# Layer 1's second-half queries projected densely and spread by four transfers, with steps 8 and 9's scores behind the transposed scores of steps 4 and 5

## What is computed

```python
x = x + L0_xattn(layernorm(x), ctx)   # 16 heads of 8
x = x + L0_ffn(layernorm(x))          # 8 experts, the best one for each token
x = x + L1_xattn(layernorm(x), ctx)   # 16 heads of 8, as below
x = x + L1_ffn(layernorm(x))          # 8 experts, the best two, gelu

q = (query @ Wq + bq); k = (key_value @ Wk + bk); v = (key_value @ Wv + bv)   # 16 heads of 8
attn = softmax(clip(q k^T * scale, -CLAMP, CLAMP))
attn = where(any(isnan(attn)), 1 / Nkv, attn)
out = (attn v) @ Wo + bo
```

## Time and profile before

| | us |
|---|---|
| median of 3 runs | 232.23 (232.05 to 233.31) |
| the profiled execution | 231.29 |
| its span in the trace | 229.5 |

### The profile page before, as it was taken

One profiled execution on the slowest core, in us unless ns is written; L12 is line 12 of the kernel. 1 busy time (PEld: TensorE's weight loads), 2 busy tenths in 40 slices (PEclk: granted clock), 3 DMA queues, 4 the chain that ended last, 5 costly groups with the idle time before them and its releaser, 6 DMA issues.

```text
span 229.5 us, 6728 instructions
## 1 busy us (share of the span) xinstructions
PE 212.9 (93%) x2522; PEld 168.8 (74%) x2522; DVE 161.1 (70%) x516; ACT 120.1 (52%) x225; POOL 75.7 (33%) x100
## 2 busy tenths in 40 slices
PE   8999987998779999999979899999699999999994
PEld 8666866766458999999875657877568686776774
DVE  1785765877556865577538755798758965799995
ACT  6765554665725655656510386567563275343340
POOL 8820810010530577646351394666600100000000
PEclk9999999999999999999999799999999999999999
DMA  6932118582244016120211110212200000001001
GB/s 216 365 110 51 50 41 276 169 282 85 58 114 95 24 60 175 50 80 26 67 51 48 50 49 28 74 50 71 76 1 0 3 0 0 3 1 46 1 3 46
DMA packets 14116, 17.18 MB, mean 75 GB/s; under 512 B 1684, under 2 KB 10004, under 8 KB 14084
## 3 DMA queue, kind: packets, MB, share of 16 engines
q1 hardware_dynamic: 11732, 13.59, 19.8%
q0 software_dynamic: 1152, 2.24, 3.2%
q10 hardware_dynamic: 1200, 0.92, 1.3%
HBM read 11.18 MB, written 3.95 MB: 66 GB/s over the span
## 4 chain that ended last, share of the span: by engine, by line
PE 71%; DVE 13%; DMA 5%; ACT 3%; issue 3%; POOL 2%; DVEq 0%; POOLq 0%; SPq 0%; ACTq 0%
PE ps L1219 12%; PE ps L1443 12%; PE ps L1455 12%; PE ps L1529 6%; PE ps L1539 5%; PE ps L1278 4%; PE ps L1227 2%; PE ps L1489 2%; DVE mx L785 2%; DVE xn L749 2%; PE ps L1316 2%; PE ps L1292 2%; PE ps L1247 2%; DMA q<-work 2%; PE ps L1180 2%
## 5 line engine op out<-in xcount | busy, mean ns | idle before, releaser
L785 DVE TENSOR_REDUCE mx<-ps 128x4 f32<-128x512 f32 x64 | 41.1, 685 | 19.7 <-PE ps L1219 19.3
L577 ACT ACTIVATE PT<-ps 128x512 f32<-128x512 f32 x64 | 35.6, 590 | 25.9 <-PE ps L1227 25.9
L1219 PE MATMUL ps<-k,q 32*128 32x128 f32 x512 | 37.0, 288 | 4.1 <-DMA q<-mT 1.2
L1219 PEld LDWEIGHTS ps<-k,q 32*128 32x128 f32 x512 | 31.4, 191 | 12.6 <-DVE mx L785 9.7
L1455 PEld LDWEIGHTS ps<-proj,work 128*128 128x128 f32 x256 | 30.7, 192 | 5.7 <-issue 5.7
L713 ACT ACTIVATE work<-ps,fc 128x512 f32<-128x512 f32 x32 | 21.4, 687 | 24.0 <-PE ps L1443 22.5
L1227 PE MATMUL ps<-q,k 32*128 32x128 f32 x512 | 33.6, 288 | 0.3 <-DVE mx L785 0.3
L1455 PE MATMUL ps<-proj,work 128*128 128x128 f32 x256 | 31.1, 275 | 0.0
L445 POOL DMA_INDIRECT moe_y<-ys,tok_i x22 | 22.3, 1012 | 24.0 <-DVE ys L1018 12.0
L1443 PE MATMUL ps<-xT,fc 128*128 128x512 f32 x64 | 30.1, 593 | 0.0
L1227 PEld LDWEIGHTS ps<-q,k 32*128 32x128 f32 x512 | 28.2, 191 | 1.0 <-issue 0.7
(11 more groups left out here) (169 smaller groups left out, 292.5 us busy)
## 6 DMA issues: line engine op xcount, KB each, us to landing
fc<-in_fc SPq DMA_DIRECT2D x8, 256.0 KB, 3.6
proj<-in_proj SPq DMA_DIRECT2D x8, 256.0 KB, 4.2
slots_x<-xs SPq DMA_DIRECT2D x2, 709.5 KB, 7.5
fc<-in_w SPq DMA_DIRECT2D x8, 129.0 KB, 2.2
proj<-in_w SPq DMA_DIRECT2D x8, 128.0 KB, 2.5
k<-work SPq DMA_DIRECT2D x12, 64.0 KB
wr<-in_wr SPq DMA_DIRECT2D x1, 719.5 KB, 7.6
xs<-slots_x SPq DMA_DIRECT2D x2, 322.5 KB, 4.0
```

The source lines that it names most:

```text
L577: nc.scalar.activation(PT[:, j % PTR, :], ps[:, ST_BANK(layer, j), :], ACT.Exp, scale=SCALE).then_inc(b_done, 1)
L785: nc.vector.tensor_reduce(mx[:, b, 4 * g:4 * g + 4], ps[:, S_BANK(layer, j), :].rearrange("p (k m) -> p k m", m=M), axis=AX, op=ALU.max).t ...
L1219: ins = mm(ps[:, S_BANK(layer, 2 * n + i), P * k:P * k + P], q4[r:r + 32, k, L * b:L * b + L], k4[r:r + 32, k, M * b:M * b + M], start=Tru ...
```

## The change

The second-half queries of layer 1 (rows 4 to 7) are projected by one dense product in step 8, evacuated once to `q_dense[:, 1, :]`, and spread by four DMAs, two issued by SP (behind the maxima of row 2) and two by ACT (behind the evacuation). In steps 8 and 9 the scores are held back: the transposed scores 4 and 5 run alone, and the scores of 8 and 9 follow behind transposed scores 5, one after the other. DVE does norm(8, 0) ahead of tops(16), and guard_count ahead of tops(18). The zero rows of q4 for rows 4 to 7, which the spaced product wrote, come by one more DMA from SP. The weights of layer 1's experts are issued one row later from expert 1 on. `wq` and `bq` of layer 1 leave the weights wr (516 columns), and qk_sums and tn2 go from 7 to 4 columns.

```diff
@@ RING
                 if layer == 1 and n == 8:
-                    for i in range(4, 8):
-                        RING[1]["q", i] = len(RING[1])
+                    RING[1]["q"] = len(RING[1])
...
+        def last_queries_in(queue, lo, hi):
+            queue.wait_ge(b_done, ring_no(1, "q"))
+            for g in range(lo, hi):
+                queue.dma_start(q4[32 * g:32 * g + DH, :, N // 2:N], q_dense[32 * g:32 * g + 32, 1, :]).then_inc(q_in[2], 16)
@@ SP, shift_rows
-                    if layer == 1 and b >= 1:
-                        expert_weights(b - 1)
+                    if layer == 1 and b == 2:
+                        last_queries_in(sp, 0, 2)
+                    elif layer == 1 and b >= 1:
+                        expert_weights(b - 1 if b < 2 else b - 2)
@@ SP
             second_keys_in(1)
+            sp.dma_start(q4[DH:P:32, :, N // 2:N], zero_rows[:]).then_inc(q_zeroed, 16)
             slots_in(1)
...
             shift_rows(1)
+            expert_weights(E - 2)
             expert_weights(E - 1)
@@ ACT
-            def queries_evac_ring(i):
-                act.wait_ge(q_ps, Q_DONE[1] + i - 3)
-                nc.scalar.activation(q4[:, i - 4, 512:1024], ps[:, ring_at(1, ("q", i)), :], ACT.Identity,
-                                     bias=wcol(1, "bq")[:, i - 4:i - 3],
-                                     accum_out=qk_sums[:, i - 1:i]).then_inc(b_done, 1)
+            def last_queries_evac():
+                act.wait_ge(q_ps, Q_DONE[1] + 1)
+                nc.scalar.activation(q_dense[:, 1, :], ps[:, ring_at(1, "q"), :], ACT.Identity, bias=wcol(1, "bqd"),
+                                     accum_out=qk_sums[:, 3:4]).then_inc(b_done, 1)
...
                     if layer == 1 and n == 8:
-                        for i in range(4, 8):
-                            queries_evac_ring(i)
+                        last_queries_evac()
+                        last_queries_in(act, 2, 4)
                         o_evac(0)
@@ DVE
                 for n in range(LAST):
+                    if layer == 1 and n == 8:
+                        norm(8, 0)
+                    if layer == 1 and n == 9:
+                        guard_count()
                     tops(2 * n)
...
-                    if layer == 1 and n == 9:
-                        guard_count()
...
-                    if n in O_T:
+                    if n in O_T and (layer, n) != (1, 8):
                         norm(n, O_T[n])
@@ PE
             def second_queries():
                 pe.wait_ge(ln_xT, XT_NO(2, 1))
-                for i in range(4, 8):
-                    pe.wait_ge(b_done, ring_no(1, ("q", i)) - 3)
-                    mm(ps[:, ring_at(1, ("q", i)), :], wcol(1, "wq")[:, P * (i - 4):P * (i - 4) + P], xT[:, 512:1024],
-                       start=True, stop=True).then_inc(q_ps, 1)
+                pe.wait_ge(b_done, ring_no(1, "q") - 3)
+                mm(ps[:, ring_at(1, "q"), :], wcol(1, "wqd"), xT[:, 512:1024], start=True, stop=True).then_inc(q_ps, 1)
...
                     if layer == 1 and n == 0:
-                        pe.wait_ge(q_zeroed, 16)
+                        pe.wait_ge(q_zeroed, 32)
                         pe.wait_ge(q_in[1], 64)
+                    if layer == 1 and n == 8:
+                        pe.wait_ge(q_in[2], 64)
...
+                def scores_alone(n):
+                    scores(n)
+                    for k in range(4):
+                        for i in range(2):
+                            score(n, i, k)
...
-                    if n < 2 * B:
+                    held = layer == 1 and n in (8, 9)
+                    if n < 2 * B and not held:
                         scores(n)
                     alone = layer == 1 and m == 0
                     if 0 <= m < 2 * B and not alone:
                         scores_t(m)
                     for k in range(4):
                         for i in range(2):
-                            if n < 2 * B:
+                            if n < 2 * B and not held:
                                 score(n, i, k)
...
+                    if layer == 1 and n == 9:
+                        scores_alone(8)
+                        scores_alone(9)
                     for j in VALUES.get(n, ()) if (layer, n) not in ((1, 6), (1, 7)) else ():
                         values(j)
```

More of the change, by code:

```diff
@@ L49 @@
 A_COLS = dict(wk=512, wkd=128, bk=4, bkd=1, bq=4, wq=512, wqd=128, bqd=1, wv=128, bv=1)
-R_COLS = dict(wo0=128, bo0=128, rw=8, wkd=128, bkd=1, wv=128, wq=512, bq=4, wqd=128, bqd=1, bv=1, wo1=128, bo1=128,
+R_COLS = dict(wo0=128, bo0=128, rw=8, wkd=128, bkd=1, wv=128, wqd=128, bqd=1, bv=1, wo1=128, bo1=128,
               wg=8, bg=8)
@@ L134, in build @@
         rstd = sb("rstd", [P, B])
-        qk_sums = sb("qk_sums", [P, 7])
+        qk_sums = sb("qk_sums", [P, 4])
         ctxsum = sb("ctxsum", [DC, B])
         vmean = sb("vmean", [P, B])
-        tn2 = sb("tn2", [P, 7])
+        tn2 = sb("tn2", [P, 4])
         nan_rows = sb("nan_rows", [P, 1])
@@ L189, in build @@
         zero_rdy, q_zeroed, q_fill = sem("zero_rdy"), sem("q_zeroed"), sem("q_fill")
-        q_in = [sem("q_in_l0b"), sem("q_in_l1a")]
+        q_in = [sem("q_in_l0b"), sem("q_in_l1a"), sem("q_in_l1b")]
         k_fill, k_in = sem("k_fill"), [sem("k_in_l0_rows23"), sem("k_in_l0b"), sem("k_in_l1a"), sem("k_in_l1b")]
@@ L501, in ln_evac @@
                 if k == 3 and half == 0:
-                    act.wait_ge(q_ps, Q_DONE[1] + 4)
+                    act.wait_ge(q_ps, Q_DONE[1] + 1)
                 bank = OUT_A_BANK if (k, half) == (3, 0) else LN_BANK[k][half]
@@ L898, in guard_count @@
             def guard_count():
-                dve.wait_ge(b_done, ring_no(1, ("q", 7)))
+                dve.wait_ge(b_done, ring_no(1, "q"))
                 link(nc.vector.tensor_tensor(tn2[:], qk_sums[:], qk_sums[:], ALU.not_equal))
@@ L1216, in score @@
                         pe.wait_ge(q_sb, k + 1)
-                    if layer == 1 and n == 8 and i == 0:
-                        pe.wait_ge(b_done, ring_no(1, ("q", 4 + k)))
                     ins = mm(ps[:, S_BANK(layer, 2 * n + i), P * k:P * k + P], q4[r:r + 32, k, L * b:L * b + L],
@@ L1625 @@
         wo0=get("L0_xattn_Wo").T[vperm], bo0=spread(get("L0_xattn_bo")), rw=get("L0_ffn_router_w").T,
-        wkd=groups(rows(get("L1_xattn_Wk"))), bkd=groups(get("L1_xattn_bk")[None]).T, wv=rows(get("L1_xattn_Wv")[:, vperm]), wq=spaced(get("L1_xattn_Wq")),
-        bq=bias4(get("L1_xattn_bq")), wqd=groups(get("L1_xattn_Wq")), bqd=groups(get("L1_xattn_bq")[None]).T,
+        wkd=groups(rows(get("L1_xattn_Wk"))), bkd=groups(get("L1_xattn_bk")[None]).T, wv=rows(get("L1_xattn_Wv")[:, vperm]),
+        wqd=groups(get("L1_xattn_Wq")), bqd=groups(get("L1_xattn_bq")[None]).T,
         bv=get("L1_xattn_bv")[vperm][:, None],
```

## The result

The changed kernel took 239.88 us (median of 4 runs, 236.80 to 239.99) against 232.14 for the kernel before (231.07 to 233.31): a ratio of 1.030, with a 95% interval of 1.020 to 1.040. The forecast was 233.1, with a range up to 235.0. So the direction that got the larger chance was right, and the size was wrong by far. The profiled execution took 239.95 us with a span of 238.2, 8.7 more than the 229.5 of before.

The account below looks back on a forecast made before the run. The prediction took the order of work on PE (71% of the chain) as the bound: 2.77 us off and 3.6 in start step 10 about 0.87 us late, which put on the median 232.23 gives 233.10 us, range 231.6 to 235.0.

Parts of the forecast that it names:

- the direction that got the larger chance: Whole kernel: slower by more than 0.5% (1.16 us) got 50%, within that 44%, faster 5% and 1 more.
- Removed: Layer 1's query projections on PE: three of four go, 3.63 us becomes 0.86, so PE loses 2.77 us.
- The lost interleaving: Steps 8 and 9 on PE: two joint steps become four halves run alone, some 2.0 us added for the halves.
- ACT's issues: Ahead of o_evac(0) in step 8: two DMA issues of 0.71 us each make PE wait 0.86 us before o_transpose.
- The landing: Query transfers ahead of scores(8): last pair issued from 137.17, wanted at 140.13, taken as hidden, so no cost.
- The prediction's upper bound: Query transfers ahead of scores(8): landing as late as GpSimd's, until 140.97, 0.84 us more; late transfers had 9%.
- The clock: Rival, 136.4 to 143 us: halves alone and waits bring PE's clock down, about 1.3 us, 234.4 in all; chance 28%.
- rows 11: Profile rows of the kernel before: PE granted 0.50, its 1.2 GHz level, from 128 to 131.5 us though busy throughout.
- The median moves as the profiled execution does: Whole kernel: the profiled execution's shift of 0.87 us was put on the median of 232.23, giving 233.10 us.
- the wr transfer, the zero transfer, the expert weights and DVE's moved pieces: Shorter R weights, one more SP zero transfer, later expert weight issues, earlier norm(8, 0) and guard_count: each 0.

Follow-up runs that it names:

- the filled kernel: Changed kernel plus three unread 0.86 us products, two ahead of step 8's o_transpose, one between scores 8 and 9: 235.36 us median, 1.022 times the kernel before.
- the two with three fillers: Changed kernel plus three unread products in steps 8 and 9, with its query transfers awaited or sent unawaited to an unread buffer: 1.022 and 1.030 times the kernel before.
- not awaited: Changed kernel with its four query transfers sent to an unread buffer and no wait for them in step 8: 1.022 times the kernel before.
- all on SP: Changed kernel with all four query transfers issued by SP, none by ACT: 14.72 us from projection to step 10, 1.028 times the kernel before.

## Why the prediction was wrong, step by step

**Removed: right in kind.** Three projections went. The one that stayed took 1.05 us until values(0), not 0.86 (136.71 to 137.76), so by PE's starts 2.6 us went, not 2.77.

**The lost interleaving: right.** 2.7 us measured at the full clock, 2.75 from the prediction's own terms, including the wait for DVE.

**ACT's issues: mis-sized.** Taken were 2 x 0.71 from SP's issues of the same shape; measured 2.26 to 2.27 us in every trace with two (1.54 for the first). The wait ahead of the o_transpose was 1.56 us, not 0.86. ACT's rows of after, with its idle time ahead of o_evac(0), and PE's row of the o_transpose:

```profile
138.68 2.27 ACTq L275 DMA_DIRECT2D q<-work  x2
141.06 0.38 ACT L597 ACTIVATE osb<-ps 128x256 f32<-128x256 f32 x1 [2.41 <-issue]
...
141.50 0.44 PE L1305 MATMUL ps<-ident,osb 128*128 128x128 f32 x2 [1.56 <-ACT osb L597]
```

Dense against spaced, with the order in both and nobody waiting for the landing, is 10.73 against 11.54, so the dense projection gives back only 0.8 us of the order's 2.7. (The two fillers ahead of the o_transpose put it 0.14 us later: from the projection, top_transpose came after 5.20 us with them and after 5.06 without. Without that it is 0.9.)

**The landing: put at nothing, and on the path.** I held 2.4 us behind the last issue for enough, from a row in which the DMA engines stood idle by then, and took the transfer as hidden. That row shows when data stopped moving; the release of a waiting engine was in no row, since nobody waited there. In the trace of after, the last packet of the four ends at 143.43, 3.2 us behind the start of the last issue (140.26), and the last update of the semaphore that PE waits for comes at 144.27; scores 8 start at 144.36, 4.1 us behind that issue. Measured are 5.6 to 5.7 us from the first issue, 1.0 of it on the path at the full clock. The prediction's upper bound, 3.8 us behind the last issue at 137.17, came to 140.97, a place 6.4 us behind the start of the path; measured were 7.65. Of these 1.2 us, 0.9 are that the last issue itself came later than forecast, and 0.3 are the landing.

With 2.7 for the order, -0.9 for dense and +1.0 for the landing, the segment is 2.8 us longer at the full clock, against 0.87 forecast. That is 11.5 us, the filled kernel's 11.78 less 0.3 for the filler (2.14 from scores 8 to 9, against 1.84). The agreement is no second proof, since the terms for dense and landing come from filled kernels too.

**The clock: the rival was right, and both its chance and its price were too low.** It got 28%, and the forecast itself put the clock at nothing. All eight traces with the dense projection and no fillers had the fall in this place; the two with three fillers had none. Which of the three did it wasn't tried. It costs 13.9 - 11.5 = 2.4 us up to step 10 and 1.2 behind it (in the other two traces 1.4 and 1.6), 3.6 in all, not 1.3. With the 2.8 above these are the 6.48 us of the two segments. So of the 5.6 us that the forecast lacked in this place, 3.6 are the clock, 1.0 the landing, and 1.0 ACT's issues (0.7) with smaller terms. I had priced two joint steps over a stretch of 3.5 us, taken from rows 11; here the low clock lasted from 143.0 to 153.3. And each us of wait that I had missed made this place thinner, so the errors may well not be independent; but the fall came without the wait for the landing too (not awaited) and without ACT's issues (all on SP), so neither alone is its cause. The range added them up only to 235.0. The rows held a warning: the same pattern, halves alone and a short wait, stood ahead of the fall in rows 11. What I set against it, four halves alone at the full level from 118.36, had no wait longer than 0.25 us among them.

**"The median moves as the profiled execution does": only roughly.** The pair of traces differs by 8.7 us, the medians by 7.7. Of the 8.7, 2.9 and -1.3 lie in stretches that the change doesn't touch, with the low clock in one trace of the two. The fall of before at 128 was in none of the other 16 traces, so its trace wasn't a typical execution there.

**Right:** that the wr transfer, the zero transfer, the expert weights and DVE's moved pieces cost nothing visible; the segment up to the router and the last one are the same within 0.05 us. The 0.53 us ahead of the first scores belong to the late start, whose cause is open.

## What to carry to other kernels

Work that keeps two halves of the array busy in turn is worth its joint time: two joint steps of 1.1 us became four halves and a bare wait for the next engine, 2.7 us, to hide a transfer that a cheaper projection had made necessary. Price a hidden transfer up to the release of someone who waited for it, not to the end of traffic: here that release came 3.8 to 4.2 us behind the start of the last issue, where 2.4 were taken. And take the issues' length from the engine that makes them. And where a change thins PE out, count the low clock as part of the likeliest case with everything behind it, and price it over the whole stretch that it may last; a few idle products in the waits, 0.86 us each here, took 4.6 us off the changed kernel, but not enough to make it worth having.

## What the runs showed of the hardware

A stretch of low clock can last much longer than the waits ahead of it: from 143.0 to 153.3 us, with PE busy for 9.0 of these 10.3 us and joint steps running again from 150.7. That isn't peculiar to the change: one trace of before had a shorter one of 3.4 us, and two others had one as long in layer 0, from 91.7 to 101.9 and from 86.6 to 96.9. The Trainium skill, TensorE: Matmul & The Clock Gate, section A second HAM failure mode: psum-queue depth-cycling, says that frequent short idles between groups can make the clock swing; this case's traces agree in part. All eight of the dense projection without fillers fell, and neither of the two with them. But what stood close ahead of the fall was, in five of the eight, the wait of 1.56 us ahead of the o_transpose, in one the same wait of 2.75, and in two the clock fell within a wait of 3.30 or 5.46 us. That the waits have to be frequent isn't shown.

ACT's first DMA issue of this shape took 1.31 us with SP idle and 1.54 beside SP, the ones behind it 0.69. Four transfers of 64 KB that together move 256 KB took 5.7 us from the first issue to PE's start over two queues and 6.5 over SP's alone. The Trainium skill, DMA: Bandwidth & Descriptors, section Issuing engines are not separate DMA queues, puts the gain of several issuing engines at the sequencer's time. That agrees: the two differ by 0.8 us, and two queues issued in 1.06 us less (2.27 against 3.33).
